# A two-layer recurrent block on one core: earlier loads at four phase seams, and one ring of three PSUM banks in the selecting attention

## What is computed

```python
# layer 0: 16 query heads, 4 key heads of width 64; two causal convolutions on q and k, rotary, causal softmax
s = L0_attention(xn); g = silu(L0_ffn(xn)); x = x + s * g
# layer 1: 32 query heads, 8 key heads of width 16, causal, and with selected chunks of 16 keys
scores = q @ k.T / 4
chunk_max = masked.reshape(..., n_chunks, 16).max(-1)
topk_idx = top_k(chunk_max, 8)
allowed = causal & (chunk in topk_idx | k_pos < 128 | k_pos > q_pos - 128)
out = softmax(where(allowed, scores, NEG)) @ v ; s = out @ wo.T
g = silu(32/16 * sum_h 8*softmax(router) * (x @ A_h.T) @ B_h.T); x = x + s * g
```

## Time and profile before

| | before |
|---|---|
| median of 3 runs | 2838.74 us (2836.09 to 2839.36) |
| the profiled execution, its own time | 2833.69 us |
| its span | 2831.9 us |
| TensorE busy, share of the span | 2417.7 us, 85% |
| VectorE | 1246.7 us, 44% |
| ScalarE | 940.6 us, 33% |
| GpSimd | 749.5 us, 26% |
| mean granted TensorE clock | 0.940 |

### The profile page before, as it was taken

The page is one execution under the profiler, slowest core; times in us unless marked ns, Lnnn a source line. Parts: engine busy times, 40 slices in busy tenths (PEclk is TensorE's granted clock), DMA queues, the critical chain, the costliest instruction groups (busy, mean ns, idle before and its releaser), DMA issues. The chain is left out here.

```text
span 2831.9 us, 46056 instructions
## 1 busy us (share of the span) xinstructions
PE 2417.7 (85%) x19426; PEld 1159.1 (41%) x19426; DVE 1246.7 (44%) x2617; ACT 940.6 (33%) x1597; POOL 749.5 (26%) x749
## 2 busy tenths in 40 slices
PE   7999859999788999999499976888578888888766
PEld 3444334444333444443255543444233333333333
DVE  2332231100043333321287772444487877787602
ACT  1111120100021111110377750222257676767630
POOL 0111001110235222223344430222343333333300
PEclk9999979999889999999699988999789999999988
DMA  6000010000222111000422204331553553444122
GB/s 215 30 30 30 15 67 15 26 26 19 101 64 63 38 41 49 16 15 16 128 83 83 83 31 163 121 121 62 112 132 60 77 75 59 59 77 75 28 93 91
DMA packets 132462, 190.33 MB, mean 67 GB/s; under 512 B 45016, under 2 KB 67288, under 8 KB 130848
## 3 DMA queue, kind: packets, MB, share of 16 engines
q1 hardware_dynamic: 130144, 183.20, 24.8%
q10 hardware_dynamic: 2112, 4.19, 0.4%
HBM read 127.05 MB, written 60.29 MB: 66 GB/s over the span
## 5 line engine op out<-in xcount | busy, mean ns | idle before, releaser
L896 PE MATMUL c_ps_c<-conv_in,c_wT 128*128 128x512 f16 x2304 | 508.4, 380 | 2.6 <-DVE c_wT L1067 2.6
L2219 ACT ACTIVATE f_probs<-f_ps_s 128x512 f32<-128x512 f32 x576 | 321.5, 596 | 136.9 <-PE f_ps_s L2123 55.6
L2337 DVE TENSOR_REDUCE f_chunk_max<-f_ps_a 128x64 f32<-128x1024 f32 x320 | 321.8, 1033 | 92.1 <-PE f_ps_a L2090 50.8
L896 PEld LDWEIGHTS c_ps_c<-conv_in,c_wT 128*128 128x128 f16 x2304 | 222.6, 98 | 279.6 <-issue 13.5
L2123 PE MATMUL f_ps_s<-f_qs,f_ks 128*32 128x512 bf16 x2304 | 218.4, 387 | 64.1 <-ACT f_probs L2219 55.5
L2090 PE MATMUL f_ps_a<-f_ka,f_qa 128*32 128x512 bf16 (+3 forms) x3072 | 200.3, 339 | 47.1 <-DMA f_v_all<-v 21.4
L1325 ACT ACTIVATE d_probs<-d_ps_s,d_shift 128x512 f32<-128x512 f32 (+3 forms) x384 | 196.5, 583 | 82.5 <-PE d_ps_s L1264 72.8
L2145 PE MATMUL f_ps_o<-f_probs,f_v 128*32 128x512 f32 (+3 forms) x1536 | 151.8, 493 | 25.7 <-ACT f_probs L2219 25.6
L624 PE MATMUL b_ps<-b_xb,b_wT 128*128 128x512 f32 x320 | 140.5, 600 | 18.0 <-DMA b_xb<-xnT 18.0
L1259 PE MATMUL d_ps_s<-d_q,d_k_high 128*64 128x512 f16 (+3 forms) x768 | 125.7, 328 | 33.0 <-DMA d_v<-v 33.0
L1275 PE MATMUL d_ps_o<-d_probs,d_v 128*64 128x512 f32 (+3 forms) x768 | 146.0, 488 | 0.0
(11 more groups left out here) (282 smaller groups left out, 3689.9 us busy)
## 6 DMA issues: line engine op xcount, KB each, us to landing
f_qa<-qk SPq DMA_DIRECT2D x96, 128.0 KB, 3.7
f_qs<-qk SPq DMA_DIRECT2D x96, 128.0 KB, 4.5
d_q<-q_parts SPq DMA_DIRECT2D x8, 1024.0 KB, 5.4
o0T<-d_stage SPq DMA_DIRECT2D x16, 512.0 KB, 2.6
e_o_in<-o0T SPq DMA_DIRECT2D x4, 2048.0 KB, 10.8
qk<-e_part SPq DMA_DIRECT2D x12, 640.0 KB, 4.9
rows<-in_qc_w SPq DMA_DIRECT2D x4, 1536.0 KB, 7.1
c_rows<-in_qc_w SPq DMA_DIRECT2D x4, 1536.0 KB, 7.7
```

What stands on the lines that cost most here:

```text
L896: last = pe.matmul(ps_c[n % 2][:], wT[m % 2][:, w, i * TAPS + a, :], conv_in[:, x, i, b, h * CH + a:h * CH + a + CH], start=(i == 0 and a ...
L2219: act.activation(probs[m % HELD][:, :, at:at + P], ps_s[n % 2][:].rearrange("p (h n) -> p h n", n=P), ACT.Exp, scale=HD1 ** -0.5).then_inc ...
L2337: dve.tensor_reduce(chunk_max[:, qt - 2, :, at:at + w // CHUNK], src.rearrange("p h (c k) -> p h c k", k=CHUNK), AX.X, ALU.max).then_inc(a ...
```

## The change

Seams. (1) In c, VectorE no longer waits for the tables before its first weights, ScalarE waits for them after `squares(0)`, TensorE before its first `sums`. (2) The loads of d's first inputs are issued in c before its last store, into the space of `conv_in`, which stays allocated until e ends. (3) The weights of e come transposed and laid out from the host, so e's transposing block is gone; they and e's tables are loaded in d, and e's first tokens are loaded in d before its last store, in the rest of `conv_in`'s space. (4) `wo` comes transposed too, and the first two loads of `o1` are issued in f before the stores of its last group; `finish_phase` no longer transposes weights.

Ring. In f, `f_ps_t` is gone and `f_ps_s` has three banks. Scores, penalties and output transposes each take the next bank in the order in which TensorE issues them, and each waits for the one three places back to be emptied by ScalarE. The turned output is therefore copied by ScalarE to a new tile `f_o_turned`, and VectorE reads it there.

```diff
@@ query_phase
+                if j == UNITS - 1:
+                    sp.wait_ge(conv_done, NCH * MQ)
+                    sp.wait_ge(stored, stored_by(j))
+                    for b in range(B):
+                        attend_inputs.load(sp, 0, b)
                 store(j)
...
+                if j == 0:
+                    pe.wait_ge(tables, 16 * 7)
...
-            act.wait_ge(tables, 16 * 7)
             weights(0)
             squares(0)
+            act.wait_ge(tables, 16 * 7)
             offsets(0)
...
         def _(dve):
-            dve.wait_ge(tables, 16 * 7)
@@ attend_phase
-            for b in range(B):
-                load(0, b)
             weights.load(sp)
...
+            for i in range(2):
+                sp.wait_ge(stored[i], 16 * (ALL // 2 - 1))
+            weights.load_tokens(sp, 0)
             store(ALL - 1)
@@ select_phase
+        SLOTS = 3
-        ps_s = [ctx.enter_context(nc.psum_tensor(f"f_ps_s{i}", [P, CH], F32)) for i in range(2)]
+        ps_s = [ctx.enter_context(nc.psum_tensor(f"f_ps_s{i}", [P, CH], F32)) for i in range(SLOTS)]
         ps_o = ctx.enter_context(nc.psum_tensor("f_ps_o", [P, CH], F32))
-        ps_t = ctx.enter_context(nc.psum_tensor("f_ps_t", [P, CH], F32))
+        o_turned = [sb(f"o_turned{i}", [P, CH]) for i in range(2)]
...
+                if g == GROUPS - 1:
+                    for half in range(2):
+                        sp.wait_ge(o_stored[half], 16 * (GROUPS - 1 + 1))
+                        inputs.load_heads(sp, half, half)
                 store(g, 0)
...
+            def next_bank(what, done, count):
+
+                if len(emptied) >= SLOTS:
+                    pe.wait_ge(*emptied[-SLOTS])
+                bank_of[what] = ps_s[len(emptied) % SLOTS]
+                emptied.append((done, count))
+                return bank_of[what]
...
-                pe.wait_ge(exp_ready, N_S * i + n + 1)
-                out, masked, part = ps_s[n % 2], kt == qt, parted(m, qt)
+                out, masked, part = next_bank(("s", i, n), exp_ready, N_S * i + n + 3), kt == qt, parted(m, qt)
...
+            def turn_out(i, half):
+                act.wait_ge(to_done, 2 * i + half + 2)
+                act.wait_ge(o_ready, 2 * i + half + 1)
+                act.activation(o_turned[half][:], bank_of["turn", i, half][:], ACT.Copy).then_inc(turned, 1)
...
             def outputs(i, half):
 
-                src = ps_t[:].rearrange("p (n c) -> p n c", c=2 * HD1)
-                dve.wait_ge(to_done, 2 * i + half + 2)
+                src = o_turned[half][:].rearrange("p (n c) -> p n c", c=2 * HD1)
+                dve.wait_ge(turned, 2 * i + half + 1)
+                dve.wait_ge(o_ready, 2 * i + half + 2)
```

More of the change, by code:

```diff
@@ L1149, in attend_phase @@
         LATE = S - KT_POOL * P
[L1150 to L1153, removed]
+        q, k_high, k_low, v, loaded, load = inputs.q, inputs.k_high, inputs.k_low, inputs.v, inputs.loaded, inputs.load
         ones = sb("ones", [P, HD0])
@@ new lines, in load, with load_tokens, tokens @@
+        sp.dma_start(self.bT[:], dram["lora_bT"]).then_inc(self.w_loaded, 16)
+        for b in range(B):
+            sp.dma_start(self.cos[:, b, :], dram["cos1"]).then_inc(self.tables, 16)
+            sp.dma_start(self.sin[:, b, :], dram["sin1"]).then_inc(self.tables, 16)
+        sp.dma_start(self.br[:], dram["lora_br"].rearrange("(a n) -> a n", a=1).to_broadcast((P, HL))).then_inc(self.tables, 16)
+    def load_tokens(self, sp, c):
+        def tokens(name):
+            return self.dram[name].rearrange("(c t p) d -> c p t d", t=TT, p=P)[ds(c, 1)].rearrange("a p t d -> p (a t) d")
+        sp.dma_start(self.o_in, self.dram["o0T"][:, :, ds(c * CH, CH)].rearrange("m p t -> p m t")).then_inc(self.loaded, 16)
+        sp.dma_start(self.g_in, tokens("g")).then_inc(self.loaded, 16)
+        sp.dma_start(self.x_in, tokens("x")).then_inc(self.loaded, 16)
@@ L2006, in second @@
             return after[n]
+        bank_of = {}
+        emptied = []
         block = ctx.enter_context(nc.Block())
@@ L2232, in attend @@
                         outputs(i, *at)
+                    elif what == "turn":
+                        turn_out(i, *at)
             def iteration(i, u, first=False):
@@ L2243, in iteration @@
                         attend(i - 1, second(n))
+                    if n == TURN1 and not first:
+                        turn_out(i - 1, 1)
             for half in range(2):
@@ L2413, in __init__ @@
         self.dram = dram
-        self.w_rows = sb("w_rows", [P, D // P, H1 * HD1])
+        self.wT = sb("wT", [P, H1 * HD1 // P, D])
+        self.o_in = [sb(f"o_in{i}", [P, TT, H1 * HD1]) for i in range(2)]
         self.g_in = [sb(f"g_in{i}", [P, TT, D]) for i in range(2)]
@@ L2480, in _ @@
             primed(pe, y_done, 2 * TT)
-            pe.wait_ge(inputs.w_loaded, 16)
-            for k in range(KO):
-                for o in range(D // P):
-                    last = pe.transpose(ps_t[k % 4][:, o * P:(o + 1) * P], w_rows[:, o, k * P:(k + 1) * P], ident[:])
-                last.then_inc(w_turned, 1)
             def turn(i, u):
```

215 lines of the change are left out of this document (89 added, 126 removed).

## The result

The changed kernel takes 2745.47 us (median of 4 runs, 2740.13 to 2752.84), the kernel before 2837.58 beside it: a ratio of 0.9677, 95% interval 0.9651 to 0.9702. That is 92 us less where 66 were forecast; the range ended at 2750. The profiled execution of after took 2742.68 us, its span 2740.9.

The account below looks back on a forecast made before the run. TensorE was taken to bound c, and TensorE and ScalarE waiting in turn to bound f. Seams of 41.1 us plus 25 for the ring gave 66, so 2838.7 − 66 = 2772 us, range 2750 to 2802.

Parts of the forecast that it names:

- Seam 1: Start of c: VectorE starts with the block, the tables' arrival hidden under the first convolution matmuls; gain 17.7 us.
- seam 2: Start of d: two loads of q, k and v issued early in c; gain 5.9 us, bounds 0 and 5.9.
- Seam 4: Start of h: weight transposes go and `o1` loads hide under f's last group; gain 5.5 us, bounds 0 and 5.5.
- Seam 3: Border d to e: transposing block goes and tokens load earlier; gain 12.0 us, bounds 0 and 12.7.
- The wrong step: Score banks in f: a third bank gains one exponential per stretch, two stretches a group, 2 × 0.60 us.
- the first rival: In f, ScalarE is simply slower, so the third bank only moves the wait to `f_ps_o`; 2798 us, chance 0.22.
- all of the wait: Upper bound in f: TensorE's whole wait for score banks goes, 15 × 3.4 + 7.0 = 58 us.
- The second penalties: In f, the score behind ScalarE's penalty copies goes when they are done, 0.65 us earlier a group.
- The copies: In f, ScalarE's two added copies a group: the first free in idle time, the second priced at 0.25 us.
- The neutral ring: Rival for f: the third bank gives nothing and only the seams pay; 2838.7 − 41.1 = 2798 us, chance 0.22.
- Copies on the path: Rival for f: every ScalarE copy costs its full time, 19.1 us, and the bank buys nothing; 2817 us, chance 0.08.
- Nearly all of the wait: Rival for f: nearly all the score-bank wait goes, if lateness does not return within a stretch; 2740 us, chance 0.05.

Follow-up runs that it names:

- experiment 8: Changed kernel, but e's first tokens loaded at the start of e's block as before, weights still transposed from the host: 2758.22 us (0.9723 of the kernel before).
- Experiment 9: Changed kernel, but VectorE waits for c's seven tables before its first weights, as before: 2761.57 us (0.9737 of the kernel before).
- Experiment 6: Changed kernel in two versions: a group's first 14 scores, or scores 14 to 24, also wait for the exponential two scores back: 2759.80 and 2753.70 us.
- experiment 5: Changed kernel, extra wait for the exponential two scores back only where the three preceding places are all scores, or only where not: 2782.19 and 2753.79 us.
- experiment 2: Changed kernel with two score banks and the separate turn bank as before, keeping the seams and ScalarE's copy of the turned output: 2796.91 us (0.9851).
- experiment 3: Changed kernel, but VectorE reads the turned output from the ring's bank and ScalarE's 32 copies are gone: 2741.12 us (0.9659 of the kernel before).
- the first kernel of experiment 6: Changed kernel, but the first 14 of a group's 36 scores also wait for the exponential two scores back: 2759.80 us (0.9732 of the kernel before).

## Why the prediction was right in sign and wrong in size

**Seams.** Right in sum, 42 against 41.1, and each by its mechanism. Seam 1's 17.8 was met to 0.1, seam 2's 5.9 too. Seam 4 gave 4.8 of 5.5. Seam 3 gave 13.1 to the start of the first project, where the forecast's terms make 12.6 to that point: 0.6 of what was taken off is the slower project behind it, which takes 29.77 us instead of 29.43, 0.3. Its step holds that the load of tokens, not the transposing, was the bound (experiment 8). The last store isn't held up by the tokens to speak of. They were issued by 1660.9, 11 us ahead of it. From the end of VectorE's last product in d to the next block it is 3.3 us (1670.68 + 1.22 to 1675.19), against 3.1 before (1695.2 to 1698.30). So the rule on the order of descriptors, for which the prediction names the Trainium skill, "DMA: Bandwidth & Descriptors", section "Queues, rings and completion order", cost 0.2 at the most here. That the sum is met within about 1 us is in part luck: single traces of one code differ by more than that.

The 2.3 us lost in c are in part the second 36 convolution matmuls: 9.64 us at a granted clock of 0.82, where they took 7.96 before. Experiment 9 shows that this is no step of the prediction that failed: most executions with the same code don't have it.

**The wrong step** is this sentence on the ring: "a third bank lets TensorE be ahead by one exponential more, once per stretch, not at each wait". The term it gave, 2 × 0.60 + 0.65 − 0.25 = 1.6 a group, measures 2.85. The sentence takes ScalarE to be behind for a whole stretch, as if its throughput set the pace. Then a lead is won once.

The ground for it was a column misread. The earlier trace rows gives PE, PEld, DVE, ACT, POOL in this order, so 486.51 us (1601 instructions) is VectorE's work in f and 401.33 (712) is ScalarE's. The prediction read 487 as ScalarE's, "close behind" TensorE's 496, and worked with "some 32 us of work in these 40.4"; it is 28.1 of 40.00 in the period shown below. The same slip stands in the first rival, where 84% should be (401 + 19) / 605.6 = 69%. The engine next in line to TensorE is VectorE, whose waits were priced at nothing.

ScalarE itself is idle for 136.9 us ahead of its exponentials, 130.0 of them for TensorE (the prediction took the row's total for one of its parts, and read 237). That line stood against the step, and was used only against a rival. The two engines wait for each other in turn: with two banks each score hangs on the exponential of the score two back, and each wait is a hand-over. The timeline of ScalarE before, in the period of the earlier trace rows:

```profile
2325.61 2.35 ACT L2219 ACTIVATE f_probs<-f_ps_s 128x512 f32<-128x512 f32 x4
2328.17 1.70 ACT L2219 ACTIVATE f_probs<-f_ps_s 128x512 f32<-128x512 f32 x3 [0.22 <-PE f_ps_s L2127]
```

The same place in the kernel after shows what a third bank makes of this:

```profile
2308.46 3.63 ACT L2200 ACTIVATE f_probs<-f_ps_s 128x512 f32<-128x512 f32 x7
2311.97 0.60 ACT L2211 ACTIVATE f_o_turned<-f_ps_s 128x512 f32<-128x512 f32 x1
2312.99 0.60 ACT L2200 ACTIVATE f_probs<-f_ps_s 128x512 f32<-128x512 f32 x1 [0.41 <-PE f_ps_s L2108]
```

Seven exponentials run without a gap, where before 0.22 us of idle time lay between four and three, and the new copy lies in the idle time that followed. Seven in a row take 3.63 us, so they start every 0.5 us though each lasts 0.60. Measured from the period's start, the kernel after is 0.93 us ahead at the copy of the first half of values (2337.47 before, 2319.39 after), 1.55 at the second turn in the period (2340.41 and 2321.71), 1.51 at the first copies of penalties (2348.40 and 2329.74), 2.42 at the last ones (2359.04 and 2339.47) and 2.85 at the end: it gains nearly everywhere. Experiment 6 shows the same by taking the lead away in parts.

**What a wait costs.** Windows of one undisturbed period, before:

```profile
2324.84:2364.84 40.00, 33.39 (x699) 15.46 (x693) 32.05 (x106) 28.11 (x50) 14.54 (x21) 1.00 0.51 70
```

and after:

```profile
2307.69:2344.84 37.15, 32.70 (x699) 15.22 (x693) 31.88 (x106) 28.03 (x52) 14.55 (x21) 1.00 0.41 70
```

TensorE has the same number of matmuls at the same clock. Its idle time falls from 6.61 to 4.45, by 2.16, and its busy time by 0.69. A group of four score matmuls lasts 0.40 us in the trace, while groups that follow each other start 0.22 apart; what doesn't overlap with a neighbour is counted as busy. So the bound "all of the wait", 3.4 a group, was itself drawn only from idle rows. With 4 waits fewer a period, each is worth an estimated 0.54 us of idle time and 0.17 of busy time. That splitting is worked out from the two rows; it wasn't tried by itself, and that the busy time falls through the overlap is argued, not shown.

**The second penalties.** The walk there was right in its mechanism and at its place: the score behind the copies now goes when they are done (2334.49, 0.97 us of wait for `f_qs`, against 1.49 at 2353.84). Measured from the period's start the lead grows there from 1.57 us at the copies to 2.20 at the score, 0.63 where 0.65 was forecast. What holding the lead at all such places costs is less, 0.39 (experiment 5), so part of a gain there is made up elsewhere.

**The copies.** Priced at 0.25 a group, they cost 0.20 in the ring and 0.00 without it. The rule of the Trainium skill, "VectorE: DVE Perf Modes", section "Rules for kernel authors", which the prediction quotes (copy "if you'll do many ops"), agrees with what the traces show of VectorE for two operations: its reciprocal takes 0.25 us from PSUM and from SBUF and the product 0.425 from both, so the copy brings VectorE nothing. That the copies then cost their whole 19 us, as the prediction worked out by the rule, is refuted by experiment 2. The version without copies is some 3 us better (experiment 3).

**The rivals.** The neutral ring (2798) is what the seams alone give, and the ring doesn't stay neutral. Copies on the path: refuted. "Nearly all of the wait" (2740, given 0.05) was the nearest, and its condition, that lateness does not return, is in the main what the runs show. It is not all of the wait, though: 31 of the 47.7 us are gone. In the rest of f, too, the gain is 6.5 where 1.2 was forecast. The prediction priced it as one group without penalties. But TensorE issues 288 score matmuls there, twice the 144 of a period, and penalties too: it is a sixteenth group beside the last choosing, and then the last group alone. Of the 7.0 us of waits for exponentials in the earlier trace rows, 1.0 are left in the same stretch, with 1.0 for penalty copies.

Open: 2 of the 15 periods before take 41.46 us. Both have a mean granted clock of 0.96, where the periods of 40.00 have 1.00, and 1.6 us more busy time of TensorE with the same work. None after is like that. What makes the clock fall in them isn't shown. The first two periods differ too (39.43 and 43.24 before, 40.32 and 38.46 after); with these f's 43.6 comes out beside 15 × 2.85 = 42.8.

## What to carry to other kernels

Before pricing another buffer between two engines, look whether the emptying engine also waits for the filling one. If it does, its throughput doesn't set the pace and the waits are hand-overs. Here a third buffer then removed 54 of 84 of them and gave 2.85 us a period, not one exponential's time per stretch. The case of an emptying engine that never idles, where one buffer's work per stretch may be right, wasn't tried. Name the column when a busy time is read from a row of windows: VectorE's 487 read as ScalarE's carried the wrong step. Work put on an engine that idles at just that place was all but free (0.00 and 0.20 us a group for two copies of 0.60), and it can be worth it to buy a bank with it. At a border between phases find the load that lands last: removing the computation above it gave nothing until that load was earlier. And before a small difference between two traces is explained, look at other traces of the same code.

## What was not expected of the hardware

Early in c the granted clock can be lower in one execution than in another of the same code. In the trace of the kernel after the second 36 convolution matmuls of 128x512 take 9.64 us at a granted clock of 0.82, between the levels of 1.2 GHz and 2.4, behind a wait of 1.90 us; so they do in the first kernel of experiment 6, behind 2.25. In ten other traces with the same code for c, and in the one before, they take 7.96, behind waits of 1.07 to 1.78. Whether the longer wait makes the clock fall isn't shown. In f the undisturbed periods repeat to 0.02 us, so that a change of 0.2 us in one of 37 can be read from a single trace, where medians of whole runs differ by several us.
